# Expert weights loaded by two DMAs with rows of 1.5 and 2 KB into padded places of the ring

## The chip, the cores and the metric

One core of one Trainium2 chip runs the whole program. The metric is the device time of one execution in microseconds, as the median of several runs; the profile is of one execution. Engines are named as the profile names them: PE (TensorE matmul), PEld (its weight loads), DVE (VectorE), ACT (ScalarE), POOL (GpSimd), SP (SyncE). SP only issues DMAs here.

## What is computed

Four layers of a transformer on 2048 tokens of width 512 in float32: attention, a mixture of 32 experts, a state-space layer, and a feed-forward layer whose weights are looked up in a table of 16. The change touches only the mixture:

```python
router_logits = x @ gate_w.T                       # 32 experts, the best 8 of each token are used
g = jnp.einsum('th,eih->tei', x, w_gate_proj)      # inner width 192
u = jnp.einsum('th,eih->tei', x, w_up_proj)
h = jax.nn.silu(g) * u * masked_w[:, :, None]
out = jnp.einsum('tei,ehi->th', h, w_down_proj)
```

## The kernel before

**Weights.** During attention POOL splits each expert's weights into a high part and a remainder, so that three products of float32r matmuls give float32 accuracy, and stores them in DRAM as `w_split`, 32 experts of 128 partitions with `W_EXPERT` = 4608 floats (18,432 bytes) each: 8 stretches of 384 floats (gate and up: 4 of the high part, 4 of the remainder) and 3 stretches of 512 floats (down: high, remainder, rest).

**Blocks.** `dispatch` sorts the chosen (token, expert) pairs by expert into 160 blocks of 128 slots. For each block it writes to `block_meta` the expert, the place of its weights in a ring of `RING` = 6 places in SBUF, and a flag that says whether the block is the first of its expert ("new"). Consecutive blocks of one expert share a place.

**The stage that the change touches** is `experts` (from L1104). All engines go through the same 160 blocks, each in its own program, coupled by semaphores:

- SP (`load`, L1145 to L1152): for block j it waits until `down` of block j-6 is done (`down_done` starts at 6), reads three numbers of `block_meta` into registers, and issues one DMA of the 2304 KB of weights into the ring (L1151). Where the block isn't new, the DMA is skipped as a whole, but its semaphore still counts. So of 160 issues 32 move data. SP has nothing else to do in this stage.
- POOL (L1158 to L1183) alternates between an indirect gather of 128 token rows of 2176 bytes (L1166, into `xg`, 16 buffers, so it runs ahead) and an indirect scatter of 128 rows of 2048 bytes that adds to the sums in DRAM (L1173). Scatter j waits for `y_done` of its block and for the landing of scatter j-2, which writes the same one of the two sums. POOL's program alternates strictly, with a scatter 12 blocks behind the gather beside it.
- PE (`step`, L1229): for block j, transpose x of block j+1 (L1194), `down` of block j-2 (L1226, 5 matmuls), transpose h of block j-1 (L1216), and `up` of block j (L1207, 12 matmuls, after `w_loaded` and `x_lo_done`).
- ACT (`step`, L1277): split x of j+1 (L1257), copy y of j-2 out of PSUM (L1275), split h of j-1 (L1263), SiLU of j (L1269), in this order. The copy of y writes one of 8 buffers, so it waits until scatter j-10 has landed (`scattered`).
- DVE (`step`, L1334): remainder of x (L1316), remainder of h (L1320), the product with the routing share (L1330, L1331), and a table look-up for the last layer in what is left of its time.

The gathers and scatters go through the profile's queue q0 (software_dynamic), SP's loads through q1 (hardware_dynamic), and ACT's two small transfers for each 16 blocks through q10. All queues are served by the same 16 DMA engines.

Of the kernel before, what the change touches and what calls it, by code (L numbers as in the profile page):

```python
# [4 lines left out]
F32 = mybir.dt.float32  # L5
# [5 lines left out]
P = 128  # L11
N_TOK = 2048
D = 512
KD = D // P
# [7 lines left out]
F32R = mybir.dt.float32r  # L22
# [26 lines left out]
def load_tokens(nc, x_in, x_res, ident):  # L49


    x_loaded = [nc.alloc_semaphore(f"x_loaded{q}") for q in range(4)]
    tiles = TILES // len(x_loaded)
    with ExitStack() as ctx:
        ident_zeroed = ctx.enter_context(nc.semaphore("ident_zeroed"))
        block = ctx.enter_context(nc.Block())

        @block.sync
        def _(sp):
            for q, loaded in enumerate(x_loaded):  # L60
                quarter = slice(q * tiles, (q + 1) * tiles)
                sp.dma_start(x_res[:, quarter, :], x_in.rearrange("(n p) d -> p n d", p=P)[:, quarter, :]).then_inc(loaded, 16)

        @block.gpsimd
        def _(pool):
            pool.memset(ident[:, :], 0.0).then_inc(ident_zeroed, 1)
            pool.wait_ge(ident_zeroed, 1)
            pool.affine_select(out=ident[:, :], in_=ident[:, :], compare_op=ALU.not_equal, fill=1.0,
                               base=0, pattern=[[-1, P]], channel_multiplier=1)
    return x_loaded  # L70
# [736 lines left out]
INTER_E = 192  # L807
REST_E = INTER_E - P
W_GU = KD * 2 * INTER_E
REST_W = D  # L810
W_RAW = W_GU + D + REST_W
HALF_W = W_GU + D
W_EXPERT = 2 * HALF_W + REST_W

SLOTS = P
BLOCKS = 160
# [2 lines left out]
RING = 6  # L819
# [108 lines left out]
def dispatch(nc, routing, chosen, x_rows, meta, block_meta, token_of, pads_ready):  # L928

    E, C, RT, B = EXPERTS, BLOCK_COLS, 8, 3  # L930
    with ExitStack() as ctx:
        sb = lambda n, s, dt=F32: ctx.enter_context(nc.sbuf_tensor("d_" + n, s, dt))
# [13 lines left out]
        expert, order, order_prev, new, turns = [sb(n, [P, C]) for n in ("expert", "order", "order_prev", "new", "turns")]  # L946
        turned_past = sb("turned_past", [P, C, RT])
        meta_i = sb("meta_i", [P, 3, C], I32)
# [7 lines left out]
        planned, plan_ready, meta_stored, meta_loaded, pads_marked = [sem(n) for n in ("planned", "plan_ready", "meta_stored", "meta_loaded", "pads_marked")]  # L956
# [67 lines left out]
        def _(dve):  # L1024
# [57 lines left out]
            dve.wait_ge(planned, 19)  # L1082
            nc.vector.scalar_tensor_tensor(meta_i[:, 1, :], turns[:, :], -float(RING), order[:, :], ALU.mult, ALU.add).then_inc(planned, 1)
            dve.wait_ge(planned, 20)
            nc.vector.tensor_scalar_mul(meta_i[:, 1, :], meta_i[:, 1, :], float(W_EXPERT)).then_inc(plan_ready, 1)

            dve.wait_ge(places_ready, 3)
            for i in range(TILES):
                if i >= B:
                    dve.wait_ge(tokens_summed, i - B + 1)  # L1090
                for k in range(TOP_K):
                    last = nc.vector.tensor_scalar(in_block[i % B][:, k, :], places[:, :], block_of[:, i, k:k + 1], token[:, i:i + 1], ALU.is_equal, ALU.mult)
# [11 lines left out]
def experts(nc, x_res, ident, x_rows, acc, block_meta, token_of, w_split, acc_ready, lut, idx, w_ffn):  # L1104
# [4 lines left out]
    BODIES = BLOCKS // U  # L1109
    NB = BLOCK_COLS * P  # L1110
    EXPERT_AT, RING_AT, NEW_AT = 0, NB, 2 * NB
    GU_HI, GU_LO, DN_HI, DN_LO, DN_REST = 0, W_GU, 2 * W_GU, 2 * W_GU + D, 2 * HALF_W
    W_UP = 2 * INTER_E
    STEPS = 19
    assert BLOCKS % U == 0 and BODIES == EARLY_LOOKUPS and LUT == 16
    with ExitStack() as ctx:
        sb = lambda n, s, dt=F32: ctx.enter_context(nc.sbuf_tensor("m_" + n, s, dt))
        ring = sb("ring", [P, RING * W_EXPERT], F32R)
        xg = [sb(f"xg{b}", [P, ROW_W]) for b in range(X_TURNS)]
        x_hi, x_lo = [sb(f"xT_hi{b}", [P, KD, P], F32R) for b in range(2)], [sb(f"xT_lo{b}", [P, KD, P], F32R) for b in range(2)]  # L1120
        silu, h = [sb(f"silu{b}", [P, INTER_E]) for b in range(2)], [sb(f"h{b}", [P, 2 * P]) for b in range(2)]
# [7 lines left out]
        ps_x, ps_u, ps_h, ps_y = pb("x", [P, KD, P]), pb("u", [P, 512]), pb("h", [P, 2, 2 * P]), pb("y", [P, D])  # L1129
        sem = lambda n: nc.alloc_semaphore("m_" + n)  # L1130
        w_loaded = [sem(f"w_loaded{b}") for b in range(U)]
# [11 lines left out]
        @block.sync  # L1143
        def _(sp):
            def load(it, b):  # L1145
                j = it * U + b
                sp.wait_ge(down_done, j + 1)
                expert = sp.value_load(block_meta[0:1, bass.ds(j + EXPERT_AT, 1)], min_val=0, max_val=EXPERTS - 1)
                place = sp.value_load(block_meta[0:1, bass.ds(j + RING_AT, 1)], min_val=0, max_val=(RING - 1) * W_EXPERT)
                new = sp.value_load(block_meta[0:1, bass.ds(j + NEW_AT, 1)], min_val=0, max_val=1)  # L1150
                sp.dma_start(ring[:, bass.ds(place, W_EXPERT)].bitcast(F32), w_split[bass.ds(expert, 1), :, :].rearrange("e p c -> p (e c)"),  # L1151
                             cond=new, bounds_check="skip_entire_dma").then_inc(w_loaded[b], 16)  # L1152

            with sp.Fori(0, BODIES) as it:
                for b in range(U):
                    load(it, b)
# [28 lines left out]
        @block.tensor  # L1185
        def _(pe):
            pe.sem_inc(down_done, RING)

            def turn_x(m, b, turn):
                pe.wait_ge(x_loaded[b], turn * 16 + 16)  # L1190
                if later(m - 1):
                    pe.wait_ge(x_lo_done, m - 1)
                for k in range(KD):
                    last = nc.tensor.transpose(ps_x[b % 2][:, k, :], xg[b][:, k * P:(k + 1) * P], ident[:, :])  # L1194
                last.then_inc(x_turned, 1)

            def ring_place(j):
                return pe.value_load(block_meta[0:1, bass.ds(j + RING_AT, 1)], min_val=0, max_val=(RING - 1) * W_EXPERT)

            def up(it, j, b, w, place):  # L1200
                pe.wait_ge(w_loaded[w], it * 16 + 16)
                pe.wait_ge(x_lo_done, j + 1)
                if later(j - 1):
                    pe.wait_ge(h_done, j - 1)
                terms = [(x_hi, GU_HI), (x_lo, GU_HI), (x_hi, GU_LO)]
                for n, (k, (x, first)) in enumerate([(k, t) for k in range(KD) for t in terms]):
                    last = nc.tensor.matmul(ps_u[b % 2][:, :W_UP], x[b % 2][:, k, :], ring[:, first + k * W_UP:][:, bass.ds(place, W_UP)],  # L1207
                                            start=(n == 0), stop=(n == 3 * KD - 1))
                last.then_inc(up_done, 1)

            def turn_h(m, b):
                pe.wait_ge(h_done, m + 1)
                if later(m - 1):
                    pe.wait_ge(h_lo_done, m - 1)
                for c in range(2):
                    last = nc.tensor.transpose(ps_h[b % 2][:, c, :P], h[b % 2][:, c * P:(c + 1) * P], ident[:, :])  # L1216
                last.then_inc(h_turned, 1)

            def down(m, b):
                place = ring_place(m)  # L1220
                pe.wait_ge(h_lo_done, m + 1)
                if later(m - 1):
                    pe.wait_ge(y_done, m - 1)
                terms = [(h_hi, 0, DN_HI), (h_lo, 0, DN_HI), (h_hi, 0, DN_LO), (h_hi, 1, DN_REST), (h_lo, 1, DN_REST)]
                for n, (a, c, first) in enumerate(terms):
                    last = nc.tensor.matmul(ps_y[b % 2][:, :], a[b % 2][:, c, :], ring[:, first:][:, bass.ds(place, D)], start=(n == 0), stop=(n == len(terms) - 1))  # L1226
                last.then_inc(down_done, 1)

            def step(it, b):  # L1229
                nxt, down_of, turn_of, own = [at(it, b, d, X_TURNS if d == 1 else TURNS) for d in (1, -2, -1, 0)]  # L1230
                if exists(own[0]):
                    place = ring_place(own[0])
                if exists(nxt[0]):
                    turn_x(*nxt)
                if exists(down_of[0]):
                    down(*down_of[:2])
                if exists(turn_of[0]):
                    turn_h(*turn_of[:2])
                if exists(own[0]):
                    up(it, *own[:2], b, place)  # L1240

            turn_x(0, 0, 0)
            for b in range(U):
                step(0, b)
            with pe.Fori(1, BODIES - 1) as it:
                for b in range(U):
                    step(it, b)
            for j in range(BLOCKS - U, BLOCKS + 2):
                step(j // U, j % U)
# [1082 lines left out]
def build_program(nc, t, out):  # L2332
    with ExitStack() as ctx:
# [3 lines left out]
        x_loaded = load_tokens(nc, t["x"], x_res, ident)  # L2337
        w_split = nc.dram_tensor("w_split", (EXPERTS, P, W_EXPERT), F32).ap()
        attention(nc, x_res, x_loaded, ident, t["w_qkv"], t["b_qk"], t["b_v"], t["wo"], t["bo"], t["w_experts"], w_split)
# [59 lines left out]
```

## Time and profile before

| | us |
|---|---|
| median of 3 runs | 2761.82 |
| lowest and highest | 2756.56, 2773.68 |
| the profiled execution's own time | 2756.39 |
| span in its profile (first to last instruction) | 2754.9 |

What lies around the span in the profiled execution is 1.5 us. The stage of the experts lies from about 857 to 1590 us of the span. A page row of the form "line engine op out<-in xcount | busy, mean ns | idle before, releaser" gives a group of instructions; idle time is named after what ended it. Windows are in us from the start of the span.

### The profile page before, as it was taken

The numbers are of one execution on the slowest core, as the hardware profiler recorded it, in microseconds if no ns is written. First come the engines' busy times: TensorE is split into PE (matmuls) and PEld (weight loads), VectorE is DVE, ScalarE is ACT, GpSimd is POOL, SyncE is SP. The second block draws the span as 40 slices with busy tenths as digits, with TensorE's granted clock in tenths as the row PEclk, the third lists the DMA queues.
The fourth block names the chain that finished last, engine by engine and source line by source line (L and its number), as shares of the span: only waits on it lengthen the run. The fifth ranks groups of instructions, "written<-read, shape, count | busy, mean of one in ns | idle before, by whom it ended". The sixth has DMA issues, their size and how long they took to land. (4 is left out here: it accounts for less than half of the span.)

```text
span 2754.9 us, 47980 instructions
## 1 busy us (share of the span) xinstructions
PE 2412.2 (88%) x12838; PEld 1830.2 (66%) x12840; DVE 1577.1 (57%) x3435; ACT 963.0 (35%) x2184; POOL 971.8 (35%) x880
## 2 busy tenths in 40 slices
PE   4978999995757999898899939999979898899997
PEld 3865555552636988887888827888855554688885
DVE  5226656662665554444445554999368786555553
ACT  3113555552144443333333412222255453222221
POOL 3127888884203555655565611211211110000000
PEclk9987999997866999999999969999999999799998
DMA  4459999995345998888898843447489550100001
GB/s 132 133 138 320 334 338 341 348 326 166 83 180 155 259 252 243 228 220 237 239 228 223 140 156 105 164 172 209 156 226 218 126 149 9 39 23 23 23 9 61
DMA packets 221836, 491.17 MB, mean 178 GB/s; under 512 B 31377, under 2 KB 115857, under 8 KB 207890
## 3 DMA queue, kind: packets, MB, share of 16 engines
q1 hardware_dynamic: 155730, 272.17, 32.2%
q0 software_dynamic: 62976, 212.42, 28.2%
q10 hardware_dynamic: 3024, 5.29, 0.6%
q8 instruction: 52, 0.85, 0.1%
q14 instruction: 54, 0.44, 0.1%
HBM read 592.96 MB, written 198.79 MB: 287 GB/s over the span
## 5 line engine op out<-in xcount | busy, mean ns | idle before, releaser
L1207 PE MATMUL m_ps_u<-m_ring,m_xT_hi 128*128 x1280 | 375.7, 355 | 0.1
L1173 POOL DMA_INDIRECT expert_sum<-x_res,token_of x160 | 254.1, 1588 | 257.8 <-ACT x_res L1275 169.5
L628 ACT ACTIVATE probs<-ps_c 128x512 f32<-128x512 f32 (+3 forms) x384 | 182.4, 490 | 215.3 <-PE ps_c L561 133.8
L1207 PEld LDWEIGHTS m_ps_u<-m_ring,m_xT_hi 128*128 128x128 f32 x1280 | 242.0, 194 | 0.9 <-issue 0.5
L658 DVE TENSOR_REDUCE neg_max<-ps_r 128x1 f32<-128x512 f32 (+3 forms) x256 | 147.7, 589 | 160.9 <-PE ps_r L528 109.1
L1226 PE MATMUL m_ps_y<-m_ring,m_hT_hi 128*128 x480 | 182.0, 434 | 55.0 <-DVE m_hT_lo L1320 48.9
L1207 PE MATMUL m_ps_u<-m_ring,m_xT_lo 128*128 x640 | 219.2, 342 | 0.0
L1166 POOL DMA_INDIRECT m_xg<-x_rows,token_of x160 | 173.1, 1082 | 103.5 <-issue 85.9
L528 PE MATMUL ps_r<-k_st,q_st 96*128 96x512 f32 (+3 forms) x384 | 163.2, 432 | 45.6 <-DVEq L651 16.9
L1643 PE MATMUL s_ps<-s_x_lo,s_w_hi 128*128 128x512 f32 x512 | 201.2, 393 | 0.0
L1643 PE MATMUL s_ps<-s_x_hi,s_w_lo 128*128 128x512 f32 x512 | 201.0, 392 | 0.0
L1643 PE MATMUL s_ps<-s_x_hi,s_w_hi 128*128 128x512 f32 x512 | 199.7, 390 | 0.0
L2309 DVE TENSOR_TENSOR x_res<-f_ps_o,x_res 128x512 f32<-128x512 f32 x176 | 109.3, 683 | 148.7 <-PE f_ps_o L2242 148.7
L1330 DVE SCALAR_TENSOR_TENSOR m_h<-m_silu,m_xg,m_ps_u 128x128 f32<-128x128 f32 x160 | 55.6, 347 | 220.1 <-ACT m_silu L1269 209.0
L1275 ACT COPY x_res<-m_ps_y 128x512 f32<-128x512 f32 x160 | 93.9, 587 | 206.5 <-PE m_ps_y L1226 111.8
L1691 ACT ACTIVATE s_out<-s_ps 128x512 f32<-128x512 f32 x128 | 76.5, 599 | 255.0 <-PE s_ps L1643 255.0
L559 PE MATMUL ps_c<-q_st,k_st 128*128 128x512 f32 (+3 forms) x384 | 157.6, 414 | 1.9 <-ACT probs L628 1.6
L572 PE MATMUL ps_y<-probs,v_pair 128*33 128x512 f32 (+3 forms) x768 | 147.9, 508 | 0.0
L1226 PEld LDWEIGHTS m_ps_y<-m_ring,m_hT_hi 128*128 128x128 f32 x480 | 92.0, 192 | 82.6 <-issue 65.4
L1320 DVE TENSOR_TENSOR m_hT_lo<-m_ps_h,m_hT_hi 128x256 fp32r<-128x256 f32 x160 | 67.4, 421 | 138.0 <-ACT m_hT_hi L1263 137.5
L1611 POOL CAST s_w_hi<-s_raw 128x512 fp32r<-128x512 f32 x32 | 22.6, 706 | 310.5 <-PE s_ps L1643 218.0
L1226 PE MATMUL m_ps_y<-m_ring,m_hT_lo 128*128 x320 | 129.3, 404 | 0.0
(335 smaller groups left out, 5783.5 us busy)
## 6 DMA issues: line engine op xcount, KB each, us to landing
m_ring<-w_split SPq DMA_DIRECT2D x160, 2304.0 KB
w_split<-e_gu_parts POOLq DMA_DIRECT2D x32, 1536.0 KB
proj<-s_out SPq DMA_DIRECT2D x32, 1024.0 KB, 3.9
e_raw_gu<-w_experts POOLq DMA_DIRECT2D x32, 768.0 KB
w_split<-e_dn_parts POOLq DMA_DIRECT2D x32, 768.0 KB
e_raw_dn<-w_experts POOLq DMA_DIRECT2D x32, 512.0 KB
q_st<-q_parts SPq DMA_DIRECT2D x32, 256.0 KB, 6.1
k_st<-k_parts SPq DMA_DIRECT2D x32, 256.0 KB, 7.1
```

Of the source, the lines that this page charges most:

```text
L528: last = nc.tensor.matmul(ps[:, :w], q_st[e][:K_QK, a, tb * P:(tb + 1) * P], k_st[e][:K_QK, a, c:c + w], start=True, stop=not diagonal)
L559: last = nc.tensor.matmul(ps_c[a][:, :width], k_st[e][:, a, s * P:(s + 1) * P], q_st[e][:, a, t0:t0 + width], start=True, stop=not diagonal)
L572: nc.tensor.matmul(ps_y[a * COL:a * COL + VW, t0:t0 + width], v_pair[e][:, a * TB + s, :], probs[a][j % RING][:, :width], start=(s == 0), ...
L628: nc.scalar.activation(probs[a][j % RING][:, :width], ps_c[a][:, :width], ACT.Exp, scale=SCALE).then_inc(exp_done, 1)
L658: nc.vector.tensor_reduce(dst, ps_r[n % 2][:, :w], AX.X, ALU.max, negate=True).then_inc(max_done, 1)
L1166: pool.indirect_dma_start(xg[j % X_TURNS][:, :], None, x_rows, rows_at(j), bounds_check=PADDED - 1, oob_is_err=True).then_inc(x_loaded[j % ...
L1173: pool.indirect_dma_start(acc[j % 2], rows_at(j), y[j % TURNS], None, bounds_check=PADDED - 1, oob_is_err=True, compute_op=ALU.add).then_i ...
L1207: last = nc.tensor.matmul(ps_u[b % 2][:, :W_UP], x[b % 2][:, k, :], ring[:, first + k * W_UP:][:, bass.ds(place, W_UP)], start=(n == 0), s ...
L1226: last = nc.tensor.matmul(ps_y[b % 2][:, :], a[b % 2][:, c, :], ring[:, first:][:, bass.ds(place, D)], start=(n == 0), stop=(n == len(term ...
L1275: nc.scalar.copy(y[b], ps_y[b % 2][:, :]).then_inc(y_done, 1)
L1643: last = nc.tensor.matmul(ps[g][:, :], w[:, k, :], x[:, k, of_group(g)], start=(n == 0), stop=(n == 3 * KD - 1))
L2309: nc.vector.tensor_tensor(x_res[:, i, :], ps_o[s][:, :], x_res[:, i, :], ALU.add).then_inc(added, 1)
```

## The change

A place of the ring gets 11 rows, each padded by 2 floats: 8 rows of 384 + 2 and 3 rows of 512 + 2, so a place is `SLOT` = 4630 floats instead of 4608. The one DMA of a block becomes two on SP's queue, under the same condition: the first has rows of 1536 bytes (8 for each partition), the second rows of 2048 bytes (3 for each partition). Each counts 16 on the same semaphore, for which `up` now waits at 32 for each block. The source in DRAM stays as it is. The matmuls read the same numbers at the new places. What `down` waits for is unchanged.

```diff
+PAD = 2
+GU_ROW, DN_ROW = 2 * INTER_E + PAD, D + PAD
+GU_ROWS, DN_ROWS = 2 * KD, 3
+SLOT = GU_ROWS * GU_ROW + DN_ROWS * DN_ROW
...
-    GU_HI, GU_LO, DN_HI, DN_LO, DN_REST = 0, W_GU, 2 * W_GU, 2 * W_GU + D, 2 * HALF_W
+    GU_HI, GU_LO, DN_AT = 0, KD * GU_ROW, GU_ROWS * GU_ROW
+    DN_HI, DN_LO, DN_REST = [DN_AT + n * DN_ROW for n in range(DN_ROWS)]
...
-                sp.dma_start(ring[:, bass.ds(place, W_EXPERT)].bitcast(F32), w_split[bass.ds(expert, 1), :, :].rearrange("e p c -> p (e c)"),
-                             cond=new, bounds_check="skip_entire_dma").then_inc(w_loaded[b], 16)
+                gate_up = ring[:, bass.ds(place, DN_AT)].rearrange("p (r c) -> p r c", c=GU_ROW)[:, :, :W_UP]
+                down = ring[:, DN_AT:][:, bass.ds(place, SLOT - DN_AT)].rearrange("p (r c) -> p r c", c=DN_ROW)[:, :, :D]
+                rows = w_split[bass.ds(expert, 1), :, :].rearrange("e p c -> p (e c)")
+                for dst, first, width in ((gate_up, 0, W_UP), (down, 2 * W_GU, D)):
+                    src = rows[:, first:first + dst.shape[1] * width].rearrange("p (r c) -> p r c", c=width)
+                    sp.dma_start(dst.bitcast(F32), src, cond=new, bounds_check="skip_entire_dma").then_inc(w_loaded[b], 16)
...
-                pe.wait_ge(w_loaded[w], it * 16 + 16)
+                pe.wait_ge(w_loaded[w], it * 32 + 32)
...
-                    ... ring[:, first + k * W_UP:][:, bass.ds(place, W_UP)],
+                    ... ring[:, first + k * GU_ROW:][:, bass.ds(place, W_UP)],
```

## Rows read from the trace of the kernel before

**Rows 1.** The page: span, busy time of the engines.

```profile
span 2754.9 us, 47980 instructions
PE 2412.2 (88%) x12838; PEld 1830.2 (66%) x12840; DVE 1577.1 (57%) x3435; ACT 963.0 (35%) x2184; POOL 971.8 (35%) x880
```

**Rows 2.** Windows: stretch, length, busy us (x instructions) by engine, clock, DMA share, GB/s.

```profile
core 0: us, PE busy (x) PEld busy (x) DVE busy (x) ACT busy (x) POOL busy (x), PEclk, DMA share, GB/s
900.00:1000.00 100.00, 99.04 (x571) 89.92 (x570) 53.48 (x124) 43.92 (x99) 52.98 (x40) 1.00 0.91 257
1000.00:1500.00 500.00, 448.33 (x2468) 402.83 (x2467) 241.24 (x562) 187.00 (x430) 284.42 (x213) 0.97 0.89 235
```

**Rows 3.** Waits of 1000 to 1500: who <- by whom: us, times, longest.

```profile
POOL expert_sum L1173 <- ACT x_res L1275: 147.9, 26, 8.1
...
DVE m_hT_lo L1320 <- ACT m_hT_hi L1263: 114.3, 72, 6.0
ACT x_res L1275 <- DMA expert_sum<-x_res,token_of: 94.7, 25, 6.7
...
PE m_ps_y L1226 <- DVE m_hT_lo L1320: 47.8, 21, 4.9
```

**Rows 4.** Timeline of ACT, 1020 to 1031: start, length, instruction [idle before].

```profile
1024.38 0.59 ACT L1257 CAST m_xT_hi<-m_ps_x 128x512 fp32r<-128x512 f32 x1
1029.38 0.58 ACT L1275 COPY x_res<-m_ps_y 128x512 f32<-128x512 f32 x1 [4.42 <-DMA expert_sum<-x_res,token_of]
...
1029.87 0.38 ACT L1263 CAST m_hT_hi<-m_ps_h 128x256 fp32r<-128x256 f32 x1
```

**Rows 5.** Landing of the scatters: first 1000 to 1500, then 1550 to 1583.

```profile
DMA to landing us min/median/max: 4.7/6.3/12.8
...
DMA to landing us min/median/max: 4.6/4.8/5.6
```

**Rows 6.** DMA view of 1016.8 to 1028.2: queues, then issues with time to landing.

```profile
q1 hardware_dynamic: 144, 2.36, 59.8%
q0 software_dynamic: 391, 0.94, 34.9%
...
expert_sum<-x_res,token_of POOLq DMA_INDIRECT x2, 12.6
m_xg<-x_rows,token_of POOLq DMA_INDIRECT x2, 10.7
```

**Rows 7.** DMA view of 1000 to 1500.

```profile
q0 software_dynamic: 23745, 57.33, 56.1%
q1 hardware_dynamic: 3456, 56.62, 30.5%
...
m_ring<-w_split SPq DMA_DIRECT2D x108, 2304.0 KB
```

**Rows 8.** Timeline of SP around 1016, and of PE from 1011.8 to 1013.8.

```profile
1016.00 0.35 SPq L1151 DMA_DIRECT2D m_ring<-w_split  x1
...
1013.32 0.40 PE L1226 MATMUL m_ps_y<-m_ring,m_hT_lo 128*128 x1
1013.55 0.38 PE L1216 MATMUL m_ps_h<-ident,m_h 128*128 128x128 f32 x2
1013.69 0.42 PE L1207 MATMUL m_ps_u<-m_ring,m_xT_hi 128*128 x1
```

**Rows 9.** DMA view of 868.0 to 872.4 (gathers alone), then 886 to 887 (a scatter alone).

```profile
q0 software_dynamic: 494, 1.72, 100.2%
...
q0 software_dynamic: 83, 0.15, 86.4%
```

**Rows 10.** DMA view of 4 to 12 (rows of 2048 bytes), then 2190 to 2195 (512 bytes).

```profile
q1 hardware_dynamic: 1586, 3.15, 103.7%
...
q1 hardware_dynamic: 709, 0.36, 27.4%
```

**Rows 11.** Page, DMA issues (KB each, us to landing), and the landings of the four loads of x_res.

```profile
a_ln_stage<-w_qkv SPq DMA_DIRECT2D x12, 256.0 KB, 2.7
...
L62 SPq DMA_DIRECT2D x_res<-x x4: 458/496/806, 1.0 to 2.6; - x4
...
DMA to landing us min/median/max: 5.7/8.9/12.2
```

More of the change, by code:

```diff
@@ L1084, in _ @@
             dve.wait_ge(planned, 20)
-            nc.vector.tensor_scalar_mul(meta_i[:, 1, :], meta_i[:, 1, :], float(W_EXPERT)).then_inc(plan_ready, 1)
+            nc.vector.tensor_scalar_mul(meta_i[:, 1, :], meta_i[:, 1, :], float(SLOT)).then_inc(plan_ready, 1)
             dve.wait_ge(places_ready, 3)
@@ L1117, in experts @@
         sb = lambda n, s, dt=F32: ctx.enter_context(nc.sbuf_tensor("m_" + n, s, dt))
-        ring = sb("ring", [P, RING * W_EXPERT], F32R)
+        ring = sb("ring", [P, RING * SLOT], F32R)
         xg = [sb(f"xg{b}", [P, ROW_W]) for b in range(X_TURNS)]
@@ L1148, in load @@
                 expert = sp.value_load(block_meta[0:1, bass.ds(j + EXPERT_AT, 1)], min_val=0, max_val=EXPERTS - 1)
-                place = sp.value_load(block_meta[0:1, bass.ds(j + RING_AT, 1)], min_val=0, max_val=(RING - 1) * W_EXPERT)
+                place = sp.value_load(block_meta[0:1, bass.ds(j + RING_AT, 1)], min_val=0, max_val=(RING - 1) * SLOT)
                 new = sp.value_load(block_meta[0:1, bass.ds(j + NEW_AT, 1)], min_val=0, max_val=1)
-                sp.dma_start(ring[:, bass.ds(place, W_EXPERT)].bitcast(F32), w_split[bass.ds(expert, 1), :, :].rearrange("e p c -> p (e c)"),
-                             cond=new, bounds_check="skip_entire_dma").then_inc(w_loaded[b], 16)
+                gate_up = ring[:, bass.ds(place, DN_AT)].rearrange("p (r c) -> p r c", c=GU_ROW)[:, :, :W_UP]
[4 more added lines that the diff above has]
+                    sp.dma_start(dst.bitcast(F32), src, cond=new, bounds_check="skip_entire_dma").then_inc(w_loaded[b], 16)
             with sp.Fori(0, BODIES) as it:
@@ L1197, in ring_place @@
             def ring_place(j):
-                return pe.value_load(block_meta[0:1, bass.ds(j + RING_AT, 1)], min_val=0, max_val=(RING - 1) * W_EXPERT)
+                return pe.value_load(block_meta[0:1, bass.ds(j + RING_AT, 1)], min_val=0, max_val=(RING - 1) * SLOT)
             def up(it, j, b, w, place):
-                pe.wait_ge(w_loaded[w], it * 16 + 16)
+                pe.wait_ge(w_loaded[w], it * 32 + 32)
                 pe.wait_ge(x_lo_done, j + 1)
@@ L1206, in up @@
                 for n, (k, (x, first)) in enumerate([(k, t) for k in range(KD) for t in terms]):
-                    last = nc.tensor.matmul(ps_u[b % 2][:, :W_UP], x[b % 2][:, k, :], ring[:, first + k * W_UP:][:, bass.ds(place, W_UP)],
+                    last = nc.tensor.matmul(ps_u[b % 2][:, :W_UP], x[b % 2][:, k, :], ring[:, first + k * GU_ROW:][:, bass.ds(place, W_UP)],
                                             start=(n == 0), stop=(n == 3 * KD - 1))
```

## The prediction

> **What bounds the kernel now.** The page comes first: PE is busy for 88% of the span, so a change matters where it makes PE wait or keeps it from waiting [rows 1]. The change touches only the stage of the experts, so I cut that stage into windows. From 900 to 1000 PE did 571 matmuls in 100 us with 99 us busy, at the full clock; from 1000 to 1500 it did 2468 in 500 us, which at 5.71 matmuls a us would take 432 us [rows 2]. These 500 us therefore lose 68 us. 51.7 us of it is idle time; the mean granted clock of 0.97 means that 0.06 of the 500 us passed at 1.2 GHz, 30 us of which half is lost, 15 us.
>
> The waits say who keeps PE standing, when read from the bottom up: PE's `down` waits 47.8 us for DVE's remainder of h, DVE 114.3 us for ACT's split of h, and ACT, whose program has the copy of y before that split, 94.7 us in 25 pieces for the landing of a scatter [rows 3]. One piece in the timeline: ACT ends its split of x at 1024.97, then sits until 1029.38 for a scatter, and only then splits h [rows 4]. The scatters land after 4.8 us (median) where no weights are loaded, at most 5.6, and up to 12.8 in the long window [rows 5]. The window of one weight load shows the collision: 144 packets of q1 (128 rows of 18,432 bytes and 16 semaphore writes) take 59.8% of the DMA engines, q0 takes 34.9%, and in it scatters land after 12.6 us, gathers after 10.7 [rows 6]. The 3456 packets of q1 from 1000 to 1500 are 24 such loads for 108 blocks [rows 7]: 25 waits of ACT for 24 loads. So 68 us are lost to 24 loads, 2.8 us each, because q0's small packets stand behind q1's big ones. POOL can't catch up quickly, since scatter j waits for scatter j-2.
>
> **What the change does to that.** Rows of 1.5 and 2 KB let the DMA engines turn to q0 after a short packet. On one engine a load's 8 packets took 0.598 x 11.4 = 6.8 us in rows 6, 0.85 us each; a row of 2048 bytes takes 1.037 x 8 x 16 / 1586 = 0.084 us, one of 512 bytes 0.274 x 5 x 16 / 709 = 0.031 us, on a straight line between them 1536 bytes take 0.066 us [rows 10]. The 8 rows of a scatter on an engine then wait behind some 8 x 0.07 = 0.6 us instead of 8 x 0.85 = 6.8 us. A scatter lands after about 5.5 to 7 us, POOL keeps up, and the 25 waits of ACT go: minus 68 us, if nothing else is late.
>
> What is late next is the load itself. **The time it has:** in PE's order `down` of block j-6 ends at 1013.72 in step j-4, just where that step's `up` starts [rows 8], and `up` of j starts four steps later; a step is 4.0 us by 571 matmuls in 100 us at 23 for a block [rows 2]. That is 16.0 us. SP's issue comes at 1016.00, 2.3 us after the `down` [rows 8], and the second DMA adds its own issue and address; SP's real issues took 0.35 to 0.5 us [rows 8, 11], I take 0.3 us (0 to 0.5). From issue to landing a load of 256 KB takes 2.7 us, of which 8 x 0.084 = 0.7 is transfer [rows 10, 11], so 2.0 us are fixed. There remain 16.0 - 2.3 - 0.3 - 2.0 = 11.4 us in which the DMA engines may work on it. Now this suffices: PE shows no wait for the ring.
>
> **The time it needs:** 64 x 0.066 + 24 x 0.084 = 6.2 us on each engine, if it had them alone. It could be 6.0 (all bytes at the price of 2048-byte rows, 72 x 0.084) or 7.4 (88 rows at that price). But q0 no longer stands back. Its own need is 64 packets for a gather, at 1.002 x 4.4 x 16 / 394 = 0.179 us (100 of the 494 packets were semaphore writes) 0.72 us for each engine, and 128 for a scatter, at 0.864 x 16 / 73 = 0.19 us 1.5 us: 2.2 us for a block [rows 9]. From the long window it is 0.561 x 500 / 108 = 2.6 us, with gaps in it that a second queue may fill [rows 7]. In 11.4 us, 2.85 blocks, q0 takes 6.3 to 7.4 us. 5.1 to 4.0 us are left for a load of 6.2: when `up` is due, 1.1 to 2.2 us of it are missing, 1.7 in the middle. While PE stands, the scatter and gather already issued (2.2 us) still share the engines; I add half of them, 1.1 us, and get a wait of 2.8 us for each load, bounds 1.1 to 4.4. It also takes PE down to 1.2 GHz now and then as today's waits do: 15 us for 24 loads, 0.6 us each. Together 3.4 to 3.5 us for each new expert. There are 31 of them behind the first, those before 1000 us too, which lose nothing today: 31 x 3.5 = 108 us added, 68 removed, net plus 40 us.
>
> **The smaller parts.** The second DMA of the 128 blocks that aren't new: SP waits for `down` anyway and has only this to do, so it costs nothing but the 0.3 us above; nothing else is queued on SP. If it made SP's turn longer than 4.0 us it would be the bound, but its turn ends 2.3 us after the `down`. The padded addresses: `up` and `down` read the same number of elements; no row prices such a start, for a matmul or for a DMA's write; I take 0, with plus 10 us as the other end (between 1 and 2% of the stage's 733 us), and nothing below 0, since no operand gets smaller. The multiplication in `dispatch` only changes its constant.
>
> A rule that speaks against two DMAs: a DMA costs about 2 us fixed, beside its bytes (the Trainium skill, "DMA: Bandwidth & Descriptors", Anatomy of one DMA). In the trace four loads of 1 MB issued within 1.6 us landed between 5.7 and 12.2 us after their issue, so 2.7 us apart, and 3.15 MB in 8 us is 2.7 us for 1 MB as well [rows 10, 11]: between DMAs of one queue nothing fixed is left. By that rule, taken for each DMA, a load would come 2 us later and the change would cost 62 us more; by the rows nothing, and the sum goes by the rows.
>
> **The sum.** The profiled execution took 2756.4 us, its span 2754.9; with plus 40 it would be 2796. The median of the runs is 5.4 us higher, so I say 2800.
>
> **The rivals.**
>
> - *The load comes in time, the scatters are early: faster.* The place is `up`'s wait for `w_loaded`; the point from which it decides is a wait (with its clock) under 2.2 us for each load, 68 / 31. For it: the lower ends above give 1.1 us and perhaps no fall of the clock, 31 x 1.1 - 68 = minus 34; and if q0's burst is put off by one scatter at the end, the wait is near 0 in many loads. Against it: even with each engine never idle, 6.2 + 6.3 us don't fit into 11.4. Time 2762 - 45 = 2717, from 2695 to 2734.
> - *A wash*, a wait of about 2.2 us: 2762.
> - *The DMA engines don't turn from queue to queue after a row.* In the trace a gather's packets hold two rows each (394 for 1.72 MB), so rows can be kept together [rows 9]. A rule says that an engine drains a whole packet, typically 9 to 17 descriptors, before it turns (the Trainium skill, "DMA: Bandwidth & Descriptors", Queues, rings and completion order). If the 8 and 3 rows of a partition stay together, packets are 12 and 6 KB and nothing much changes: 2762 again. The trace counts the hardware queue's rows one by one (1586 packets for 3.15 MB), so I give this little.
> - *Each turn between queues costs.* A row of 18,432 bytes took 0.85 us beside q0, where 9 x 0.084 is 0.76. 0.09 us for a turn. A load has 88 rows instead of 8; if some half of them alternate with q0, 40 x 0.09 = 3.6 us more: a wait of 6.4 and a clock of 0.6, 31 x 7.0 - 68 = plus 149, 2911. Against it: the gathers alone ran at 100% of the engines with packets of 0.18 us [rows 9], so short packets as such cost nothing beside their own time.
>
> **How the numbers follow.** Forecast (PE waits some 3 us for each load) 0.38; the price of turns 0.12; wash 0.14; rows that stay together 0.06; faster 0.30. A measurement tells about 1% from no change, 28 us. Slower by over 1% is the forecast and the price of turns, 0.50; within 1% the wash and the rows together, 0.20; faster 0.30. The range goes from the faster rival's own time, 2715, to the upper ends of the forecast's terms: load 7.4, q0 7.4 (missing 3.4), all of the 2.2 still in the queue and the clock, 6.2 us, 31 x 6.2 - 68 = plus 124, 2890. The forecast's own range is 2790 to 2890.
>
> **What would show it.** In the profile after: q1 with 88 packets for each engine instead of 8, so over 1400 for a load; the landing of scatters from 1000 to 1500 at most about 7 us; the wait of ACT's L1275 for a DMA gone or small; in its place PE's L1207 waiting for a DMA into m_ring (or, without a name, "issue"), some 30 times for 2 to 4 us. I am wrong if L1207 has no such wait, if the scatters still land after 12 us, or if SP's issues come more than 3 us after `down`.

## The result, and the profile after

| | before | after |
|---|---|---|
| median, us | 2761.03 (6 runs) | 2733.99 (6 runs) |
| lowest and highest | 2756.56, 2773.68 | 2730.05, 2743.86 |
| the profiled execution | 2756.39 | 2730.05 |

The ratio is 0.9901, with an interval of 0.9876 to 0.9926: 27 us faster, a gain of about 1%. The forecast was 2800, plus 40 us. The time lies inside the range, but on the side of the first rival.

The page after, span and busy time (columns as in [rows 1]):

```profile
span 2728.5 us, 48628 instructions
PE 2405.0 (88%) x12838; PEld 1821.6 (67%) x12840; DVE 1576.5 (58%) x3435; ACT 968.6 (35%) x2184; POOL 975.3 (36%) x880
```

PE does the same 12,838 matmuls and still fills 88%; the gain is idle time and clock. The windows of the stage after, columns as in [rows 2]:

```profile
857.00:1000.00 143.00, 122.06 (x664) 109.76 (x665) 65.63 (x154) 52.23 (x116) 84.77 (x66) 0.90 0.88 247
1000.00:1500.00 500.00, 478.34 (x2709) 430.72 (x2710) 260.61 (x609) 209.83 (x471) 316.57 (x236) 1.00 0.95 253
```

and the first of them in the kernel before:

```profile
857.00:1000.00 143.00, 132.63 (x752) 120.49 (x753) 72.44 (x169) 58.87 (x130) 80.28 (x63) 0.95 0.91 262
```

Read them by the matmuls. From 1000 to 1500 there are 2709 instead of 2468: 241 more, 42 us of work at 5.71 matmuls a us. From 857 to 1000 there are 664 instead of 752: 88 fewer, 15 us given back. The difference is the 27 us. So the change gains where loads and scatters collide and loses at the start of the stage. From the first transposition of x to the last `down`, a measure that does not hang on where the stage begins, the stage takes 696.0 us instead of 726.8; some 4 us of that are lost again behind it, and by what stays open.

The waits from 1000 to 1500 after, against [rows 3]:

```profile
POOL expert_sum L1182 <- ACT x_res L1284: 70.4, 52, 3.9
POOL expert_sum L1182 <- DMA expert_sum<-x_res,token_of: 41.5, 22, 4.2
DVE m_hT_lo L1329 <- ACT m_hT_hi L1272: 40.5, 60, 1.9
...
PE m_ps_u L1216 <- DMA m_ring<-w_split: 14.6, 11, 2.3
...
PE m_ps_y L1235 <- issue: 4.5, 12, 0.8
```

ACT's copy of y (L1284, before L1275) has no line for a DMA any more; it was 94.7 us in 25 pieces. (A line without a name, "issue", has 10.5 us in 15 pieces, so at most that much is left.) Scatters still come late (POOL waits 41.5 us in 22 pieces for the scatter two back, where before that was 3.3 us), but never by so much that the 8 buffers of y run out, and only that reaches ACT. PE's `up` (L1216) now waits for the load, as forecast, but 14.6 us in 11 pieces, and not some 30 times for 2 to 4 us. Over the whole stage (857 to 1700) PE's lines show the exchange. After ("busy, mean ns | idle before, by releaser"):

```profile
L1216 PE MATMUL m_ps_u<-m_ring,m_xT_hi 128*128 x1280 | 372.1, 352 | 31.9 <-DMA m_ring<-w_split 19.8 <-issue 10.7 <-DVE m_xT_lo L1325 1.2
...
L1235 PE MATMUL m_ps_y<-m_ring,m_hT_hi 128*128 x480 | 178.6, 426 | 6.3 <-issue 5.0 <-DVE m_hT_lo L1329 1.1
```

Before:

```profile
L1207 PE MATMUL m_ps_u<-m_ring,m_xT_hi 128*128 x1280 | 375.7, 355 | 0.1
...
L1226 PE MATMUL m_ps_y<-m_ring,m_hT_hi 128*128 x480 | 182.0, 434 | 55.0 <-DVE m_hT_lo L1320 48.9 <-issue 5.6
```

55.1 us of idle time ahead of `up` and `down` became 38.2. 10.3 of these are one piece, ahead of the very first `up`; it has no name in the profile, but ends 1.0 us after the last packet of the first load.

The DMA view of 1000 to 1500 after, against [rows 7]:

```profile
q0 software_dynamic: 26372, 63.61, 58.0%
q1 hardware_dynamic: 36000, 58.99, 34.8%
...
m_ring<-w_split SPq DMA_DIRECT2D x117, 1536.0 KB
```

One load alone is 1440 packets (128 x 11 rows and 32 semaphore writes), the 88 rows for each engine that were predicted; 36,000 packets are 25 loads. They take 0.348 x 500 / 25 = 7.0 us of each engine for a load, where 6.2 was estimated. q0 takes 0.580 x 500 / 118 = 2.5 us for a block.

A load in detail, first SP's two issues and PE's step around them, then the DMA view of 1017.5 to 1030.8:

```profile
1014.31 0.38 PE L1225 MATMUL m_ps_h<-ident,m_h 128*128 128x128 f32 x2
...
1017.32 0.85 SPq L1161 DMA_DIRECT2D m_ring<-w_split  x2
...
1031.21 0.43 PE L1216 MATMUL m_ps_u<-m_ring,m_xT_hi 128*128 x1 [0.56 <-DMA m_ring<-w_split]
```

```profile
q1 hardware_dynamic: 1440, 2.36, 54.0%
q0 software_dynamic: 629, 1.49, 45.2%
```

Both issues take 0.85 us; `up` was due at 1030.65, 13.3 us after the first, which is about what the forecast had given it (16.0 - 2.3 - 0.3 = 13.4). The load's packets run from 1018.05 to 1030.51, so 0.7 us after the first issue to 0.7 us before `up`, which starts 0.56 us late. In these 12.5 us they take 7.2 us of each engine, q0's packets 5.7. The engines are full for most of it: from 1020.5 to 1024 q1 has 52.5% and q0 55.3% (packets overlap, so the shares can pass 100% together), while from 1017.5 to 1019.5 only q1's packets run, with 54%.

The same for all 25 loads that begin between 1000 and 1500: the first packet comes 1.1 us (median) after SP's issue, the packets run for 11.0 to 14.3 us, 12.3 in the mean, in which the load takes 7.0 us of each engine and q0 5.5, and where `up` waits it starts 0.7 us (median) after the last of them. From the issue to the time at which `up` is due there are 13.8 us in the mean. So a load is in time or late by a little, as its packets run for less or more than some 12 us. In the longest wait of the stretch `up` starts 2.30 us after it was due, with another queue's 4.5% beside it (1245.5 to 1261.0, q10 is ACT's transfers):

```profile
q0 software_dynamic: 744, 1.84, 48.7%
q1 hardware_dynamic: 1440, 2.36, 46.8%
q10 hardware_dynamic: 144, 0.26, 4.5%
```

```profile
1260.80 0.44 PE L1216 MATMUL m_ps_u<-m_ring,m_xT_hi 128*128 x1 [2.30 <-DMA m_ring<-w_split]
```

The 15 us at the start of the stage are 10.6 us of busy time that PE lacks (122.06 instead of 132.63) and matmuls that take longer. The first `up` comes at 873.49 instead of 867.88. The first load, beside a burst of gathers that hold 52.4% of the engines (857.5 to 872.5, where the load takes 44.9%), no longer takes the larger part: its packets run for 13.7 us, before for 8.5. Before:

```profile
867.88 0.68 PE L1207 MATMUL m_ps_u<-m_ring,m_xT_hi 128*128 x1
```

After, with a later one of the same stretch:

```profile
873.49 0.68 PE L1216 MATMUL m_ps_u<-m_ring,m_xT_hi 128*128 x1 [10.28 <-issue]
...
918.21 0.68 PE L1216 MATMUL m_ps_u<-m_ring,m_xT_hi 128*128 x1 [3.29 <-DMA m_ring<-w_split]
```

The latter took 0.68 us where such a matmul takes 0.43 elsewhere: after 3.29 us without work PE stands at 1.2 GHz for a while (granted clock 0.50 from 918.2 to 922). It is the longest of four such waits between 900 and 1000, 5.7 us in all. The mean clock of 857 to 1000 fell from 0.95 to 0.90. After the short waits behind 1000 it did not fall (1.00).

### The profile page after: what moved, and what is told of

It reads as the page before. It is cut to its first block and busy times, and to the rows that moved or that the text cites. A ratio compares the mean times of both kernels' runs of the same rounds, so it can differ in the third digit from the quotient of the medians.

```text
span 2728.5 us, 48628 instructions
## 1 busy us (share of the span) xinstructions
PE 2405.0 (88%) x12838; PEld 1821.6 (67%) x12840; DVE 1576.5 (58%) x3435; ACT 968.6 (35%) x2184; POOL 975.3 (36%) x880
## 5 line engine op out<-in xcount | busy, mean ns | idle before, releaser
L1216 PE MATMUL m_ps_u<-m_ring,m_xT_hi 128*128 x1280 | 372.1, 352 | 31.9 <-DMA m_ring<-w_split 19.8
L1216 PEld LDWEIGHTS m_ps_u<-m_ring,m_xT_hi 128*128 128x128 f32 x1280 | 237.6, 190 | 37.1 <-issue 36.7
L1216 PE MATMUL m_ps_u<-m_ring,m_xT_lo 128*128 x640 | 217.6, 340 | 0.0
L1278 ACT ACTIVATE m_silu<-m_ps_u 128x192 f32<-128x192 f32 x160 | 53.0, 331 | 274.4 <-PE m_ps_u L1216 192.7
L1284 ACT COPY x_res<-m_ps_y 128x512 f32<-128x512 f32 x160 | 94.0, 588 | 106.9 <-PE m_ps_y L1235 95.7
L2009 PE MATMUL s_ps_o<-s_w_out_sb,gated 128*128 128x512 f32 x256 | 126.9, 623 | 1.3 <-DVE gated L2146 1.3
```

The lines of the kernel that those rows point to most:

```text
L2009: last = nc.tensor.matmul(ps_o[tt][:, :], gated[b][:, k, tt * P:(tt + 1) * P], w_o[:, k, :], start=(k == 0), stop=(k == KO - 1))
```

## The experiments

**The theory after the result:** two deadlines share one resource. The scatter's (8 buffers of y) was missed before; the load's (`up`, four steps after the place is free) is missed now, by a little. **The rivals:** that splitting the load and its second issue do it, not the short rows; that the row only has to be some size below 18 KB; that the start of the stage is the main loss. The stretch of 1000 to 1470 is used for all kernels, since the fastest of them are near the end of the stage by 1500. The kernels ran on several chips, on which the one before took 2757 to 2761 us (medians), so medians of different sections compare to within some 4 us; each ratio is to the kernel before on the same chip. Before and after in it:

```profile
1000.00:1470.00 470.00, 422.48 (x2321) 379.46 (x2320) 226.03 (x528) 175.82 (x404) 269.60 (x202) 0.96 0.89 235
```

```profile
1000.00:1470.00 470.00, 449.62 (x2546) 404.75 (x2546) 247.47 (x577) 197.37 (x443) 297.61 (x221) 1.00 0.96 259
```

### Is it the rows, or the split?

Without the padding the rows of each DMA lie side by side on both ends and count as one: 12,288 and 6144 bytes.

```diff
-PAD = 2
+PAD = 0
```

> The changed kernel without its padding: two DMAs, whose rows for one partition lie end to end, so that they should go as rows of 12,288 and 6144 bytes. Theory (short rows let the scatters through; two DMAs as such do nothing): the gain goes, 2755 to 2770 us, scatters' packets again late by 5 us during a load, ACT's copy of y waits for scatters again. Rival (issuing the load in two halves is what helps): 2735 us, as the changed kernel.

Measured: 2737.69 us, ratio 0.9915 (0.9887 to 0.9944). The time is the rival's, not the theory's 2755 to 2770: two DMAs without short rows gain as much. But the gain is made otherwise, as window and waits of 1000 to 1470 show:

```profile
1000.00:1470.00 470.00, 437.02 (x2426) 392.19 (x2425) 236.51 (x552) 184.49 (x423) 277.78 (x207) 0.97 0.90 243
```

```profile
ACT x_res L1284 <- DMA expert_sum<-x_res,token_of: 81.2, 28, 5.9
...
PE m_ps_y L1235 <- DVE m_hT_lo L1329: 27.5, 20, 4.1
```

Here the scatter waits remain, each shorter (2.9 us instead of 3.9 in the mean), and nobody waits for the load there. In this window it does 2426 matmuls, 120 fewer than the changed kernel, 21 us. But it loses less at the start, where it does 716 from 857 to 1000 (the changed kernel 664, the one before 752), 9 us, although its stage begins 5.5 us later: the first `up` comes 10.0 us after the first transposition, in the changed kernel 14.2, in the one before 8.4. The whole stage takes 704.2 us, 8 us more than in the changed kernel. These 8 and the later start, which is not of the change, are the 14 us by which the two profiled executions differ (2744.30 and 2730.05); the medians differ by only 4.

The next kernel has one DMA for each load again, in three padded rows of 6144 bytes:

```diff
-GU_ROW, DN_ROW = 2 * INTER_E + PAD, D + PAD
-GU_ROWS, DN_ROWS = 2 * KD, 3
+ROW, ROWS = W_GU + PAD, 3
+SLOT = ROWS * ROW
...
-                pe.wait_ge(w_loaded[w], it * 32 + 32)
+                pe.wait_ge(w_loaded[w], it * 16 + 16)
```

> One DMA of three padded rows of 6144 bytes for each partition, so 24 rows for each DMA engine instead of 88 (changed kernel) or 8 (before). A row of 6144 bytes takes some 0.24 us, so the 8 rows of a scatter wait about 2 us more in a load, not 7: scatters land after 7 to 8 us. Theory (alternation row by row): scatters are still in time for POOL's turn of two blocks (8 us) and the load gets a bigger share, so it ends earlier than with short rows and the waits of up for the ring shrink: 2715 to 2735 us, at most as long as the changed kernel. Rival (only rows of 2 KB and less let q0 through): near 2760 us.

Measured: 2733.04 us, ratio 0.9898 (0.9868 to 0.9927). The waits of 1000 to 1470:

```profile
ACT x_res L1280 <- DMA expert_sum<-x_res,token_of: 74.6, 27, 4.6
```

The time is what the theory gave, and the scatter waits are what it did not give: they are shorter, not gone (2.8 us each). So neither the second DMA (this kernel has one) nor a row below 6 KB is needed for this gain, and the kernels with rows between 12 KB and 1.5 KB take 2733 to 2738. At 12 KB the row and the second DMA came together; no run separates them there. With one wait for the whole load, shorter rows move time from one wait to the other.

### Relaxing the load's deadline

`up` needs gate and up of the new expert; `down` needs its own part two steps later. With its own semaphores the second DMA gets these two steps (about 8 us) more. Both sets are 8 semaphores, each used twice in a round of 16 blocks:

```diff
-        w_loaded = [sem(f"w_loaded{b}") for b in range(U)]
+        w_loaded, down_loaded = [[sem(f"{n}_loaded{b}") for b in range(TURNS)] for n in ("w", "wd")]
...
-                pe.wait_ge(w_loaded[w], it * 32 + 32)
+                pe.wait_ge(w_loaded[w % TURNS], (it * 2 + w // TURNS) * 16 + 16)
...
-            def down(m, b):
+            def down(m, b, w, turn):
...
+                pe.wait_ge(down_loaded[w], turn * 16 + 16)
```

> The changed kernel, but the second DMA counts on semaphores of its own, for which down waits, two steps after up. up then waits only for the first 64 of the 88 rows of each engine. Theory (what is left of the cost is up's wait for the end of the load, some 20 us of idle PE from 1000 to 1470 in the changed kernel): these waits go, since the last quarter of a load takes about 3 us and the waits are up to 2.3 us: 2705 to 2720 us. Rival (another thing keeps the steps at 4.26 us for a block, such as full DMA engines or waits for gathers): within 5 us of the changed kernel, 2734.

Measured: 2704.95 us, ratio 0.9808 (0.9787 to 0.9829), as the theory expected: 29 us below the changed kernel by the medians, 26 by the ratios, 23 by the profiled executions. Window and waits:

```profile
1000.00:1470.00 470.00, 457.15 (x2602) 412.05 (x2601) 251.42 (x585) 201.11 (x452) 306.06 (x229) 1.00 0.98 261
```

```profile
POOL expert_sum L1182 <- DMA expert_sum<-x_res,token_of: 56.2, 19, 5.0
...
PE m_ps_u L1216 <- DMA m_ring<-w_split: 5.9, 5, 1.5
PE m_ps_y L1236 <- issue: 5.8, 16, 0.6
```

PE's wait for the load falls from 13.3 us in 10 pieces (changed kernel, same stretch) to 5.9 in 5, with the same bytes in the same rows. In this stretch it does 56 matmuls more than the changed kernel, 10 us. As much comes from the start: from 857 to 1000 it does 727 instead of 664, 11 us, and its first `up` comes 10.0 us after the first transposition instead of 14.2, since it waits only for gate and up of the first load. 0.98 of the DMA engines' time is taken. The scatters land after 6.1 us (median), at most 10.4: not the 7 us predicted, and harmless all the same: ACT waits for no scatter by name. That PE hardly waits here matters for the reading of the changed kernel, because PE's waits for loads alone can also take ACT's waits away, as the section on the deadline shows; here, with PE's waits at 5.9 us, it is the short rows that do it.

The same with no padding tells whether the two waits alone do it:

> The kernel with a wait of its own for the second DMA (2705 us), but without the padding, so rows of 12,288 and 6144 bytes. It tells whether short rows are worth anything once the load has more time. Theory (with long rows the loss is ACT's wait for scatters, with short ones up's wait for the load, and the two waits help only against the second): the scatters stay late, 2730 to 2745 us, like the unpadded kernel with one wait (2738). Rival (the separate wait is the whole gain): 2700 to 2712 us.

Measured: 2733.20 us, ratio 0.9905 (0.9875 to 0.9934), 28 us above the padded one (26 us in the stage of the profiled executions). Its waits:

```profile
ACT x_res L1285 <- DMA expert_sum<-x_res,token_of: 87.3, 28, 4.7
...
PE m_ps_y L1236 <- issue: 32.8, 28, 2.8
```

A later deadline for the load is worth little while the scatters' is the one that is missed: 4 us against one wait, with overlapping intervals. `down`'s 28 waits have no name here ("issue"), but come beside ACT's 28 for scatters, which end before the split of h as in [rows 4].

With two waits, rows of 6144 bytes (two for gate and up, one for down), and rows of 3072 bytes for gate and up with 2048 for down (the edit of the second):

```diff
-GU_ROW, DN_ROW = 2 * INTER_E + PAD, D + PAD
-GU_ROWS, DN_ROWS = 2 * KD, 3
+GU_ROW, DN_ROW = 4 * INTER_E + PAD, D + PAD
+GU_ROWS, DN_ROWS = KD, 3
```

> The same two waits, with rows of 6144 bytes in both DMAs (two rows, padded, and one). Theory: scatters still stand behind rows of 0.25 us, so between the two: 2715 to 2735 us, with ACT still waiting for scatters. Rival: 2700 to 2712 us, if 6 KB is short enough when the load's end isn't waited for.

Measured: 2716.74 us, ratio 0.9852 (0.9830 to 0.9874), within the theory's 2715 to 2735. ACT still waits for scatters, 67.9 us in 24 pieces. Against the same rows with one wait and one DMA this is 16 us less, so a later deadline of the load is of use here even beside these waits; 26 matmuls more from 857 to 1000 (4.6 us) and 47 more from 1000 to 1470 (8 us) make most of it.

> Two waits, gate and up in 4 padded rows of 3072 bytes instead of 8 of 1536; the down rows stay at 2048 bytes. It tells whether shorter is always better: so far, with two waits, rows of 12 and 6 KB gave 2733, 6 KB 2717, 1.5 and 2 KB 2705 us. Theory (what counts is how long a scatter's row stands behind one load row, 0.12 us here, while 32 rows fewer for each engine shorten the load by some 0.3 us): 2703 to 2712 us, about as the short rows. Rival (a scatter's lateness falls in proportion to the row): 2708 to 2712 us, slower than 1.5 KB by more than 3 us.

Measured: 2699.78 us, ratio 0.9781 (0.9757 to 0.9804), the fastest kernel of the study, 61 us below the one before. Both the theory (2703 to 2712) and its rival (2708 to 2712) had expected more. Its window:

```profile
1000.00:1470.00 470.00, 463.47 (x2648) 418.85 (x2647) 256.66 (x599) 204.86 (x462) 308.01 (x230) 1.00 0.97 260
```

Against rows of 1.5 KB the medians differ by 5 us, with overlapping intervals of the ratio: the trace favours 3 KB (46 more matmuls, 8 us; `up` waits 0.5 us once for a load in this stretch), the times alone don't settle it. From 857 to 1000 it does 742 matmuls, so all but 10 of the 88 that the changed kernel loses there are back. The table of all row lengths, medians in us:

| rows, bytes | one wait | two waits |
|---|---|---|
| 18,432 | 2761 | |
| 12,288 and 6144 | 2738 | 2733 |
| 6144 | 2733 | 2717 |
| 3072 and 2048 | | 2700 |
| 1536 and 2048 | 2734 | 2705 |

Down the right column short rows gain 28 to 33 us; down the middle one they gain nothing behind the first step. The short rows are worth their gain only with a load that may be late.

### What the collision costs in all

In the kernel before, "new" holds for block 0 only, and every block reads place 0. This leaves out 31 of the 32 loads, and the experts' sums are of wrong weights; the work of the engines stays:

```diff
-... scalar_tensor_tensor(meta_i[:, 2, :], block_no[:, :], 0.0, new[:, :], ALU.is_equal, ALU.add) ...
+... scalar_tensor_tensor(meta_i[:, 2, :], block_no[:, :], 0.0, one[:, :C], ALU.is_equal, ALU.mult) ...
...
-            ... tensor_scalar_mul(meta_i[:, 1, :], meta_i[:, 1, :], float(W_EXPERT)) ...
+            ... tensor_scalar_mul(meta_i[:, 1, :], meta_i[:, 1, :], 0.0) ...
```

> The kernel before, but only the first block's weights are loaded and all blocks use that place of the ring (31 of 32 expert loads are left out, so the sums of the experts are of wrong weights). It gives the floor: what all loads but the first cost the kernel before, hidden and not. Theory: 68 us of 1000 to 1500 and a few before, so 2680 to 2695 us, with a step of 3.93 us throughout and no wait of ACT for scatters. Rival (POOL's own turn of 3.3 us and the scatters' latency already hold the steps back without loads): above 2710 us.

Measured: 2682.60 us, ratio 0.9731 (0.9713 to 0.9750). Its window:

```profile
1000.00:1470.00 470.00, 467.59 (x2705) 426.51 (x2704) 261.45 (x613) 208.72 (x470) 314.00 (x234) 1.00 0.76 143
```

PE hardly waits (2.4 us from 1000 to 1470): this is the floor. The 76 us between it and the kernel before on its chip (2758.72) are the whole price of loading beside the scatters; the change takes 27 of them, the 3 KB rows with two waits 61, and some 15 remain. In the window it does 384 matmuls more than before, 67 us.

### Is the deadline really tight?

SP issues each load one step later (about 4 us), once in the changed kernel and once in the one before:

```diff
-                sp.wait_ge(down_done, j + 1)
+                sp.wait_ge(down_done, j + 2)
```

> The changed kernel, but SP issues each load when down of block j-5 is done instead of j-6, one step of some 4 us later, so the load has that much less time. Theory (in the changed kernel the load ends just when up wants it, its slack is 0.8 us after the last packet, which is only the landing): each of 31 loads makes up wait some 3 to 4 us more, less what the freed DMA engines give back: 2800 to 2850 us. Rival (the load had spare time): under 2760 us.

Measured: 2892.63 us, ratio 1.0498 (1.0475 to 1.0522), more than the 2800 to 2850 of the theory. Window and wait:

```profile
1000.00:1470.00 470.00, 385.60 (x1976) 350.80 (x1977) 189.27 (x441) 152.04 (x342) 228.14 (x172) 0.88 0.74 202
```

```profile
PE m_ps_u L1216 <- DMA m_ring<-w_split: 85.0, 20, 6.6
```

> The same edit in the kernel before. There the load's last packet ends 2 to 9 us before up wants it, so a step less costs little: some loads of the first blocks wait 1 to 3 us, and every wait gives the scatters time to catch up. Theory: 2760 to 2785 us, far less than the changed kernel loses. Rival (its loads have no more time to spare than the changed one's): over 2800 us.

Measured: 2784.64 us, ratio 1.0115 (1.0087 to 1.0143). Its waits, in which ACT no longer waits for any scatter:

```profile
PE m_ps_u L1207 <- DMA m_ring<-w_split: 41.0, 19, 3.4
```

The same 4 us cost 159 us in the changed kernel (by medians of two chips; 165 by the ratios) and 28 in the one before (2784.64 - 2756.69, on the same chip, inside the theory's 2760 to 2785). 159 / 31 is 5.1 us for each load, more than the 4 us of delay: the waits, now 85.0 / 20 = 4.2 us each, come with PE at 1.2 GHz for about a quarter of the time (clock 0.88). So the changed kernel has no slack left at this point, and the one before, whose waits are 41.0 / 19 = 2.2 us each, had some 2 us in hand.

The second kernel also shows the exchange from the other side, with rows of 18,432 bytes: once PE waits for loads, ACT's waits for scatters go, although scatters still land after up to 13.3 us. From 1000 to 1500 PE is idle for as long as before (52.5 us, before 51.7) and does as many matmuls (2460, before 2468); the costs replace each other there rather than add up. The 28 us are lost mainly at the start, where it does 661 matmuls from 857 to 1000 instead of 752, 16 us. That PE's wait gives the scatters their time is the likely reason and is not tested by itself. It follows that the missing wait of ACT in a profile does not yet show that the scatters are early.

### The start of the stage

On the kernel with two waits, POOL's third gather waits for the first load:

```diff
+                if j == 2:
+                    pool.wait_ge(w_loaded[0], 16)
```

> The kernel with two waits and short rows (2705 us), but POOL issues the gathers of blocks 2 and later only when the first gate and up weights have landed. In the changed kernel the first load shares the DMA engines with 16 gathers and takes 13.7 us, and the first up starts at 873.5 instead of 867.9. Theory: the first up starts 5 to 8 us earlier and this stays, 2697 to 2701 us. Rival (the gathers and the first scatters are then late and take it back): 2703 to 2710 us.

Measured: 2705.53 us, ratio 0.9806 (0.9784 to 0.9829), against 2704.95 without it; the theory had 2697 to 2701, the rival 2703 to 2710. The first `up` starts at 863.69, 7.3 us after the first transposition instead of 10.0, and then PE stands again:

```profile
863.69 0.68 PE L1218 MATMUL m_ps_u<-m_ring,m_xT_hi 128*128 x1 [2.95 <-DMA m_ring<-w_split]
...
879.16 0.69 PE L1227 MATMUL m_ps_h<-ident,m_h 128*128 128x128 f32 x2 [5.70 <-issue]
```

What PE lacks at 879.16 is h, not gathered rows: it transposed the next x at 871.51 without a wait. h waits for ACT's SiLU, which starts at 878.02 after 8.06 us of idle time that the profile puts down to no instruction of the core ("remote"). Why it stood is open. From 857 to 1000 there are 724 matmuls, without the edit 727: this way of sharing the start gained nothing.

## Why the prediction was wrong

**What bounds the kernel: right.** Of the 68 us said to be lost to the loads from 1000 to 1500, the kernel without loads regains all: it does 2881 matmuls there, 413 more, 72 us. The changed kernel regains 42 and still loses 500 - 2709 / 5.71 = 26.

**ACT's 25 waits go, minus 68 us: right in mechanism, too large in size.** They go, but 26 us are still lost, of which 14.6 are the load's. The scatters' own part was wrong (at most 7 us, against 10.4 with the same rows and two waits), and did not matter: what is needed is only that none is later than the 8 buffers of y cover.

**Who is late next: right.** It is `up` at `w_loaded`, and the time that it has from SP's issue, 13.4 us, is about what the trace shows (13.8 in the mean). SP's issue comes 2.75 us (median) after `down`, said were 2.3 + 0.3; one load, at 3.1, passed the 3 us that were to be a sign of being wrong.

**The step that failed: the wait of each load, "1.7 in the middle ... I add half of them, 1.1 us, and get a wait of 2.8 us".** Measured are 14.6 us for the 25 loads from 1000 to 1500, 0.6 us each. In the forecast's terms a load's packets were to run for 6.2 + 6.9 + 1.1 = 14.2 us where there are 11.4. They run for 12.3 us (mean of the 25 loads) where there are 13.8 - 1.1 - 0.7 = 12.0. Term by term:

- q0's share, 6.3 to 7.4 us, was too large: beside a load q0 takes 5.5 us. I gave it the whole of its usual need for 2.85 blocks; in the trace the two queues take about half each, and q0 catches up afterwards (from 1029 to 1030.8, where the load shown ends, q0 has 98%).
- The added 1.1 us for half of the queued burst has nothing that answers to it: the load's last rows are not behind that burst.
- The load's own need was too small, 7.0 us where 6.2 were said.
- The time there is was 0.6 us too small; of this 0.3 us are the fixed ends (2.0 said, 1.1 + 0.7 measured).

The first two take 2.5 us from the wait, the third puts 0.8 back, the fourth takes 0.6. The lower bound, 1.1, was the one without the added burst, and even it was too high in the mean. Since both sides are about 12 us and a load's packets run for 11.0 to 14.3 us, some loads are late by up to 2.3 us and the others not at all. These sizes are read from the trace; no run changes one of them alone.

**The clock, 0.6 us for each load: wrong for the 25, not before 1000.** It was carried over from a kernel in which PE's waits were 47.8 / 21 = 2.3 us in the mean and up to 4.9 (clock 0.97). Waits of up to 2.3 us, 1.3 in the mean, leave the granted clock at 1.00 from 1000 to 1500. With waits of 4.2 us it is 0.88. From 857 to 1000, with the 10.3 and the 3.29 us, it is 0.90, before 0.95. The clock's cost should have hung on the length of the waits in the same sum.

**"Those before 1000 us too, which lose nothing today": right, and it is where the change loses.** 15 us are lost there. A good third is not in the sum at all: it counts the 31 loads behind the first, and the first, whose packets run 5 us longer than before, puts the first `up` off by 5.6 us. The other six make PE wait 5.7 us, about 1 us each. With 15 us for the 25 loads and 15 for the start the step's sum would have been 30 - 68 = minus 38. The measured minus 27 is less, since of the 26 us still lost in the long window only 14.6 are by name the load's; the rest is 7 us of other waits, mostly of `down`, and 4 us of slightly longer matmuls.

**The smaller parts: right.** 1440 packets for a load; no sign of a price for padded addresses: the mean matmul of `up` is 352 ns, 355 before.

**The rivals.** *The load comes in time* is nearest to what came about, though not as it was told: loads do come late, 2734 is the upper end of its own times (2695 to 2734), and 27 us is just under the 28 from which a change was to be told from none. Its condition, wait and clock under 2.2 us for each load, held with room (0.6), and its chance of 0.30 was too low for a condition that lay inside the forecast's own bounds of 1.1 to 4.4. *Rows that stay together* is refuted by the kernels with two waits: with packets of 12 and 6 KB ACT waits 87.3 us for scatters, with the short rows not at all, so these do not act as packets of 12 and 6 KB. (ACT's missing wait in the changed kernel would not do as proof, by the section on the deadline.) Its time was wrong as well: with packets of 12 and 6 KB and one wait the kernel takes 2738 us, not 2762. *The price of turns* is not seen: a load takes 7.0 us of each engine for 88 rows beside q0, at most 0.8 us above the estimate, not 3.6. The rule on 2 us fixed for each DMA (the Trainium skill, "DMA: Bandwidth & Descriptors", Anatomy of one DMA, where it stands for DMAs that GpSimd issues) did not act between the two DMAs of a load: in none of the 25 loads is q1 without a packet for more than 0.16 us between the first and the last. The 1.1 and 0.7 us at the two ends come once for each load.

**Settled and open.** Settled: that the deadline of the load is what the change trades against (one step later, 159 us), that short rows keep ACT from waiting for scatters, and that more of the gain lies behind a later deadline (two waits, 29 us by the medians, nearly half of it at the start). Most of the start's 15 us can be had: 11 with two waits, 14 with rows of 3 KB. Open: why beside a load q0 takes 5.5 us and not its usual need, and what keeps ACT after the first load in the last experiment.

## What to carry to other kernels

A transfer that waits behind another's big rows and a transfer that has a deadline of its own are one problem: cutting the rows takes from one what it gives to the other. Before cutting, find the deadline of both; where the big transfer holds parts that are used at different times, give each its own semaphore first, and then cut (29 us more here than cutting alone, by the medians). And when a wait is forecast as a difference of two nearly equal times (11.4 had, 12.5 needed), its sign is the forecast: give the two sides equal chances and look at what each costs, instead of adding a surcharge to the middle.

## What was not expected of the hardware

Cutting a row from 18,432 to 12,288 bytes, with the load in two DMAs, was already worth 1%, as much as cutting it to 1536; rows of 6144 bytes in one DMA gave the same. A load took 0.305 x 500 / 24 = 6.4 us of each engine with rows of 18,432 bytes [rows 7] and 7.0 with rows of 1536 and 2048, so 11 times as many rows cost a tenth. Waits of PE up to 2.3 us stood before no matmul at 1.2 GHz in the rows shown (0.44 us for the first), the one of 3.29 us did (0.68).
